# Three pairwise additions in place of one summing operation over the eight state terms

## The reference, cut to what matters

```
kv[i, j] = k[i] * v[j]                         # 8 x 8 products; here k = v, so 36 distinct pairs
out[i, j] = causal_conv(kv[i, j], kernel[h]) + kv[i, j] * D[h]
result[j] = sum over i = 0..7 of out[i, j] * q[i]
```

## Time and profile before

| what | value |
|---|---|
| median of 3 runs | 2442.73 us (2441.63 to 2445.28) |
| the profiled execution, its own time | 2441.71 us |
| its span, first to last instruction | 2439.9 us |
| busy in the span: PE, DVE, POOL | 2141.1 (88%), 1535.5 (63%), 949.3 us (39%) |
| mean granted TensorE clock | 0.936 |
| the summing operation, L1575 | 128 times, 267.3 us |

### The profile page before, as it was taken

The page is one execution under the profiler, slowest core; times in us unless marked ns, Lnnn a source line. Parts: engine busy times, 40 slices in busy tenths (PEclk is TensorE's granted clock), DMA queues, the critical chain, the costliest instruction groups (busy, mean ns, idle before and its releaser), DMA issues.

```text
span 2439.9 us, 32911 instructions
## 1 busy us (share of the span) xinstructions
PE 2141.1 (88%) x10954; PEld 1674.5 (69%) x10994; DVE 1535.5 (63%) x2567; ACT 1031.8 (42%) x1427; POOL 949.3 (39%) x774
## 2 busy tenths in 40 slices
PE   5989468888888645899999999999999999999898
PEld 4978445545455334688788688688688688688677
DVE  4866457776776558387488378478478477477411
ACT  3345344455545321533633543533533543443333
POOL 0100122333322021464464365365375375375263
PEclk9999789999999956799999999999999899999899
DMA  6656311111110021222322232232232232222231
GB/s 221 225 188 224 115 45 65 69 69 69 55 44 35 23 74 44 69 88 73 96 82 81 82 93 83 76 97 83 76 100 82 73 103 74 81 81 57 69 100 60
DMA packets 85161, 214.90 MB, mean 88 GB/s; under 512 B 7632, under 2 KB 9040, under 8 KB 79840
## 3 DMA queue, kind: packets, MB, share of 16 engines
q1 hardware_dynamic: 84800, 214.01, 26.8%
q10 hardware_dynamic: 288, 0.09, 0.0%
HBM read 180.52 MB, written 33.55 MB: 88 GB/s over the span
## 4 chain that ended last, share of the span: by engine, by line
PE 47%; issue 6%; DVE 6%; ACT 3%; POOL 2%; DMA 1%; ACTq 0%; SPq 0%; DVEq 0%; POOLq 0%
PE e_ps_u L52 4%; PE e_ps_u L53 4%; PE e_ps_u L54 4%; PE e_ps_out L52 4%; PE e_ps_out L54 4%; PE e_ps_out L53 4%; PE e_ps_g L52 3%; PE e_ps_g L53 3%; PE e_ps_g L54 3%; PE e_ps_m L52 3%; PE e_ps_m L54 3%; PE e_ps_m L53 3%; PE e_ps_m L1753 1%; DVE e_x3T L1575 1%; DVE e_kv_lo L1547 1%
## 5 line engine op out<-in xcount | busy, mean ns | idle before, releaser
L1232 POOL TENSOR_TENSOR e_gu_lo<-e_gu_raw,e_gu_hi 128x1024 fp32r<-128x1024 f32 (+1 forms) x128 | 272.0, 2125 | 414.1 <-ACT e_gu_hi L1315 412.3
L1575 DVE TENSOR_REDUCE e_x3T<-e_zp 128x128 f32<-128x1024 f32 x128 | 267.3, 2088 | 4.4
L1515 DVE SCALAR_TENSOR_TENSOR e_hd<-e_ps_u,vecs,e_sgw 128x512 f32<-128x512 f32 x96 | 71.9, 749 | 279.0 <-POOL e_sgw L1246 169.2
L52 PE MATMUL e_ps_out<-e_hd_hi,e_dn_hi 128*128 128x512 f32 x512 | 209.6, 409 | 0.0
L52 PE MATMUL e_ps_u<-e_xn_hi,e_gu_hi 128*128 128x512 f32 x512 | 209.0, 408 | 0.6 <-DVE e_hd L1515 0.6
L53 PE MATMUL e_ps_u<-e_xn_lo,e_gu_hi 128*128 128x512 f32 x512 | 206.0, 402 | 0.0
L54 PE MATMUL e_ps_u<-e_xn_hi,e_gu_lo 128*128 128x512 f32 x512 | 205.7, 402 | 0.0
L54 PE MATMUL e_ps_out<-e_hd_hi,e_dn_lo 128*128 128x512 f32 x512 | 204.9, 400 | 0.0
L53 PE MATMUL e_ps_out<-e_hd_lo,e_dn_hi 128*128 128x512 f32 x512 | 204.4, 399 | 0.0
L52 PE MATMUL e_ps_m<-e_kv_hi,e_t_hi 128*128 128x288 f32 x592 | 179.6, 303 | 22.6 <-DVE e_kv_lo L1547 16.9
L1237 POOL TENSOR_TENSOR e_dn_lo<-e_dn_raw,e_dn_hi 128x512 fp32r<-128x512 f32 x128 | 174.4, 1363 | 40.3 <-ACT e_dn_hi L1321 40.3
(11 more groups left out here) (288 smaller groups left out, 5417.5 us busy)
## 6 DMA issues: line engine op xcount, KB each, us to landing
e_gu_raw<-in_mgu SPq DMA_DIRECT2D x96, 512.0 KB, 3.3
e_dn_raw<-in_md SPq DMA_DIRECT2D x128, 256.0 KB, 3.1
stage<-in_x SPq DMA_DIRECT2D x8, 1024.0 KB, 6.9
c<-in_ctxT SPq DMA_DIRECT2D x8, 1024.0 KB, 5.6
raw_w<-in_w1T SPq DMA_DIRECT2D x8, 1024.0 KB, 4.8
raw_w<-in_w2T SPq DMA_DIRECT2D x8, 1024.0 KB, 7.4
gates<-gate SPq DMA_DIRECT2D x8, 1024.0 KB, 4.8
vals<-val SPq DMA_DIRECT2D x8, 1024.0 KB, 3.9
```

Of the source, the lines that this page charges most:

```text
L52: nc.tensor.matmul(out, w_hi, x_hi, start=first, stop=False, skip_group_check=skip)
L1232: nc.gpsimd.tensor_tensor(gu_lo[:, s % 2, a], gu_raw[:, s % 2, a], f32(gu_hi[:, s % 2, a]), ALU.subtract).then_inc(gulo_done, 1)
L1515: nc.vector.scalar_tensor_tensor(out=hd[:], in0=ps_u[:], scalar=vecs[:, V_BU + s:V_BU + s + 1], in1=sgw[:], op0=ALU.add, op1=ALU.mult).the ...
L1575: nc.vector.tensor_reduce(x3T[:, lb].rearrange("p (b n) -> p b n", b=B)[:, :, hh * CD:(hh + 1) * CD], zv(5, (1, 8), (21, 8)), AX.X, ALU.ad ...
```

## The change

The reduction of L1575 becomes three tensor additions on the same tile: four pairs of terms in place (512 numbers per partition), two pairs in place (256), and one pair into x3T (128). A new semaphore, tree_done, orders them. All eight terms lie in zp as before. Elsewhere the diff only merges semaphores that one engine counts up in a row, with the waits' numbers changed to match; no instruction other than the sum is added, removed or moved.

```diff
@@ experts_block, vector engine, unit()
             dve.wait_ge(prod_done, START + 4 * (v + 1))
-            nc.vector.tensor_reduce(x3T[:, lb].rearrange("p (b n) -> p b n", b=B)[:, :, hh * CD:(hh + 1) * CD],
-                                    zv(5, (1, 8), (21, 8)), AX.X, ALU.add).then_inc(red_done, 1)
+            nc.vector.tensor_tensor(zv(5, (21, 4), (1, 8)), zv(5, (21, 4), (1, 8)), zv(5 + 84, (21, 4), (1, 8)), ALU.add).then_inc(tree_done, 1)
+            dve.wait_ge(tree_done, START + 2 * v + 1)
+            nc.vector.tensor_tensor(zv(5, (21, 2), (1, 8)), zv(5, (21, 2), (1, 8)), zv(5 + 42, (21, 2), (1, 8)), ALU.add).then_inc(tree_done, 1)
+            dve.wait_ge(tree_done, START + 2 * v + 2)
+            nc.vector.tensor_tensor(x3T[:, lb].rearrange("p (b n) -> p b n", b=B)[:, :, hh * CD:(hh + 1) * CD],
+                                    zv(5, (1, 8)), zv(5 + 21, (1, 8)), ALU.add).then_inc(red_done, 1)
...
@@ setup_block: ghi_done is merged into hi_done
-        dve.wait_ge(ghi_done, 1)
+        dve.wait_ge(hi_done, len(cuts) + 1)
...
@@ scores_block: mask_done, abs_done, ahi_done become mask_step
-            dve.wait_ge(mask_done, h + 1)
+            dve.wait_ge(mask_step, 3 * h + 1)
...
@@ attn_block: amax_done is merged into qs_done, hmax_done into hs_done
-            act.wait_ge(qs_done, 10 * q + 5 * a + 5)
+            act.wait_ge(qs_done, 12 * q + 6 * a + 6)
...
-            act.wait_ge(hs_done, 4 * (4 * c + j + 1))
+            act.wait_ge(hs_done, 5 * (4 * c + j + 1))
```

More of the change, by code:

```diff
@@ L80, in setup_block @@
     ps_g = st.enter_context(nc.psum_tensor("ps_g", [P, 512], F32))
-    vecs_in, ident_in, wh_in, wht_in, wg_in, hi_done, lo_done, g_done, ghi_done = (
-        sem(n) for n in ("vecs_in", "ident_in", "wh_in", "wht_in", "wg_in", "hi_done", "lo_done", "g_done", "ghi_done"))
+    vecs_in, ident_in, wh_in, wht_in, wg_in, hi_done, lo_done, g_done = (
+        sem(n) for n in ("vecs_in", "ident_in", "wh_in", "wht_in", "wg_in", "hi_done", "lo_done", "g_done"))
     cuts = [(raw_wht, wht_hi, wht_lo, wht_in), (raw_wh, keep["wh_hi"], keep["wh_lo"], wh_in),
@@ L103, in _ @@
         act.wait_ge(g_done, 1)
-        nc.scalar.activation(keep["g_hi"][:], ps_g[:].rearrange("p (h d) -> p h d", h=HEADS), ACT.Copy).then_inc(ghi_done, 1)
+        nc.scalar.activation(keep["g_hi"][:], ps_g[:].rearrange("p (h d) -> p h d", h=HEADS), ACT.Copy).then_inc(hi_done, 1)
     @block.gpsimd
@@ L160, in scores_block @@
     names = ("x_in c_in stats_done mom_done rstd_done shift_done xn_done chi_done clo_done filled xhi_done qhi_done xnT_done "
[L161 removed]
+             "val_done gate_done q_done scores_done consts_done val_out gate_out mask_step const_in "
              "w1_in w2_in wohi_done wolo_done part_done sum_done mean_done scale_done scaled_done clip_done tern_done v0_in")
     (x_in, c_in, stats_done, mom_done, rstd_done, shift_done, xn_done, chi_done, clo_done, filled, xhi_done, qhi_done, xnT_done,
[L164 removed]
+     val_done, gate_done, q_done, scores_done, consts_done, val_out, gate_out, mask_step, const_in,
      w1_in, w2_in, wohi_done, wolo_done, part_done, sum_done, mean_done, scale_done, scaled_done, clip_done, tern_done, v0_in) = (
@@ L396, in _ @@
             dve.wait_ge(scores_done, START + HEADS * (NCH - 1) + h + 1)
-            nc.vector.tensor_tensor(gate[:, h], acc[:, h], keep["mask"][:, h], ALU.mult).then_inc(mask_done, 1)
-            dve.wait_ge(mask_done, h + 1)
+            nc.vector.tensor_tensor(gate[:, h], acc[:, h], keep["mask"][:, h], ALU.mult).then_inc(mask_step, 1)
+            dve.wait_ge(mask_step, 3 * h + 1)
             nc.vector.scalar_tensor_tensor(out=val[:, h], in0=gate[:, h], scalar=-1.0, in1=gate[:, h], op0=ALU.mult,
[L400 to L403, removed]
+                                           op1=ALU.max).then_inc(mask_step, 1)
+            dve.wait_ge(mask_step, 3 * h + 2)
+            nc.vector.tensor_scalar(keep["at_hi"][:, h], val[:, h], 1.0, None, ALU.max).then_inc(mask_step, 1)
+            dve.wait_ge(mask_step, 3 * h + 3)
             nc.vector.scalar_tensor_tensor(out=keep["at_lo"][:, h], in0=val[:, h], scalar=1.0, in1=f32(keep["at_hi"][:, h]),
@@ L506, in attn_block @@
      oT_done, og_done, z_done, zhi_done, zlo_done, wo_done, x1_done, stats_done, mom_done, rstd_done, rms_step,
-     r2_done, y_done, yg_done, amax_done, qs_done, round_done, yq_done, t_done, t_read, h_done, gelu_done,
-     hmax_done, hs_done, hround_done, hq_done, mm2_done, x2_done, x2_out, consts_done, dq2w_done, shift_done, held_done) = (sem(n) for n in (
+     r2_done, y_done, yg_done, qs_done, round_done, yq_done, t_done, t_read, h_done, gelu_done,
+     hs_done, hround_done, hq_done, mm2_done, x2_done, x2_out, consts_done, dq2w_done, shift_done, held_done) = (sem(n) for n in (
          "v_in gate_in x_in vhi_done vlo_done o_done ostats_done omom_done orstd_done oshift_done on_done "
          "oT_done og_done z_done zhi_done zlo_done wo_done x1_done stats_done mom_done rstd_done rms_step "
-         "r2_done y_done yg_done amax_done qs_done round_done yq_done t_done t_read h_done gelu_done "
-         "hmax_done hs_done hround_done hq_done mm2_done x2_done x2_out consts_done dq2w_done shift_done held_done").split())
+         "r2_done y_done yg_done qs_done round_done yq_done t_done t_read h_done gelu_done "
+         "hs_done hround_done hq_done mm2_done x2_done x2_out consts_done dq2w_done shift_done held_done").split())
     TU = 2 * TJ + 2
@@ L790, in pair_scale @@
             cols = slice(2 * a, 2 * a + 2)
-            n = 10 * q + 5 * a
+            n = 12 * q + 6 * a
             dve.wait_ge(yg_done, 4 * q + 2 * a + 2)
-            nc.vector.tensor_reduce(amax[:, cols], y[:, cols], AX.X, ALU.max, apply_absolute_value=True).then_inc(amax_done, 1)
-            dve.wait_ge(amax_done, 2 * q + a + 1)
+            nc.vector.tensor_reduce(amax[:, cols], y[:, cols], AX.X, ALU.max, apply_absolute_value=True).then_inc(qs_done, 1)
+            dve.wait_ge(qs_done, n + 1)
             nc.vector.tensor_scalar(amax[:, cols], amax[:, cols], 1e-5, None, ALU.max).then_inc(qs_done, 1)
-            dve.wait_ge(qs_done, n + 1)
+            dve.wait_ge(qs_done, n + 2)
             nc.vector.reciprocal(qrec[:, cols], amax[:, cols]).then_inc(qs_done, 1)
             nc.vector.tensor_scalar(dq1[:, cols], amax[:, cols], 1.0 / QMAX, keep["wmean"][:, 0:1], ALU.mult, ALU.mult).then_inc(qs_done, 2)
-            dve.wait_ge(qs_done, n + 4)
+            dve.wait_ge(qs_done, n + 5)
             nc.vector.tensor_scalar(qscale[:, cols], qrec[:, cols], QMAX, None, ALU.mult).then_inc(qs_done, 1)
@@ L815, in scale_h @@
             dve.wait_ge(gelu_done, START + 16 * c + 4 * j + 4)
-            nc.vector.tensor_reduce(hmax[:, col], h[:, j % 2], AX.X, ALU.max, apply_absolute_value=True).then_inc(hmax_done, 1)
-            n = 4 * (4 * c + j)
-            dve.wait_ge(hmax_done, 4 * c + j + 1)
+            nc.vector.tensor_reduce(hmax[:, col], h[:, j % 2], AX.X, ALU.max, apply_absolute_value=True).then_inc(hs_done, 1)
+            n = 5 * (4 * c + j)
+            dve.wait_ge(hs_done, n + 1)
             nc.vector.tensor_scalar(hmax[:, col], hmax[:, col], 1e-5, None, ALU.max).then_inc(hs_done, 1)
-            dve.wait_ge(hs_done, n + 1)
+            dve.wait_ge(hs_done, n + 2)
             nc.vector.reciprocal(hrec[:, col], hmax[:, col]).then_inc(hs_done, 1)
             nc.vector.tensor_scalar(dq2[:, col], hmax[:, col], dq2w[:], None, ALU.mult).then_inc(hs_done, 1)
-            dve.wait_ge(hs_done, n + 3)
+            dve.wait_ge(hs_done, n + 4)
             nc.vector.tensor_scalar(hscale[:, col], hrec[:, col], QMAX, None, ALU.mult).then_inc(hs_done, 1)
@@ L1642, in finish @@
                                                op1=ALU.add).then_inc(y_done, 1)
-        for s in (hdlo_done, stt_done, kvlo_done, tlo_done, prod_done, red_done, x3_done, xn_done, lg_done, wT_done, y_done):
+        for s in (hdlo_done, stt_done, kvlo_done, tlo_done, prod_done, tree_done, red_done, x3_done, xn_done, lg_done, wT_done, y_done):
             dve.sem_inc(s, START)
```

4 lines of the change are left out of this document (2 added, 2 removed).

## The result

The changed kernel takes 2469.35 us (median of 4 runs, 2464.37 to 2471.81) against 2442.18 us of the kernel before (4 runs). The ratio is 1.0108, 95% interval 1.0089 to 1.0126: 27 us, or 1.1%, slower. The forecast was 2459.5 us, range 2436 to 2484, with a chance of 0.65 for slower.

The account below looks back on a forecast made before the run. The DVE was taken to bound the opening, the PE the rounds. The opening's -7.0 us and the rounds' +23.8 made +16.8 us on the median 2442.73, about 2459.5 us, range 2436 to 2484.

Parts of the forecast that it names:

- The price alone: Every unit: three additions hold the DVE 1.40 us against the sum's 1.92, gaining 0.52 us where nothing interferes.
- Rival 3: Additions cost 2 ns a number like the strided reduction; opening loses 13 to 20 us, time about 2504; chance 0.07.
- the 1.0 for units 6 and 14: Opening: two units where the DVE already waits for the PE, so 2 by 0.52 us of gain comes off.
- The 0.3 taken off for the matrix cuts: Opening: 0.3 us less gain for three matrix cuts, where ACT waits for the PE as well.
- The mechanism: Rounds: operations with two SBUF inputs exclude each other, so each addition takes turns with POOL's; 3.4 us lost a round.
- The walk of steps 4 to 5: Rounds: additions queue behind POOL's operations, hd_lo ends at 1066.0, and PE's down of step 4 starts 1.1 us late.
- The walk of steps 7 to 8: Rounds: unit 7's additions queue behind POOL, so unit 8's products reach PE's unit 9 0.9 to 2.2 us late; 1.5 taken.
- late branch: Unit 7 to 8: POOL's sgw comes ahead of kv_lo, so unit 8's products end at 1101.3, 2.2 us late.
- For the rest ... I set 0.8 us, a choice and not a walk: Rounds: loss of 0.8 us a round set for units 1, 2, 5 and 11 to 13.
- rival 1: The rounds' margins absorb all delays and only the opening's gain counts: 2436 us; chance 0.17.
- rival 2: Turns fall well, about 1 us lost a round, 7 in all, cancelling the opening: 2438 to 2447 us; chance 0.18.
- rival 4: The same turns with POOL, but heavier: above 5.5 us a round, 2475 to 2490 us; chance 0.1.

## Why the prediction was right

**The pace.** The split into an opening paced by the DVE and rounds paced by the PE held. The kernel with neighbour reads shows both halves at once: 0.9 us less DVE time in every unit gave 11 us in the opening and left PE's wait for the products in the rounds, and the 107.9 us of the unit span, as they were.

**The price alone.** 0.69, 0.43 and 0.29 us were forecast and found. The opening's timeline shows the chain:

```profile
891.56 0.28 DVE L1572 TENSOR_TENSOR e_zp<-e_ps_m,e_qe 128x144 f32<-128x144 f32 x1
891.88 0.69 DVE L1575 TENSOR_TENSOR e_zp<-e_zp 128x512 f32<-128x512 f32 x1
892.61 0.43 DVE L1577 TENSOR_TENSOR e_zp<-e_zp 128x256 f32<-128x256 f32 x1
893.07 0.29 DVE L1579 TENSOR_TENSOR e_x3T<-e_zp 128x128 f32<-128x128 f32 x1
893.28 0.75 DVE L1547 TENSOR_TENSOR e_kv_lo<-e_kv_raw,e_kv_hi 128x576 fp32r<-128x576 f32 x1
```

893.28 - 891.88 = 1.40 us, the forecast to the hundredth. Rival 3 (2 ns a number) is refuted: these additions of runs of eight neighbours don't pay for the 84 bytes between the runs. The rule for reductions in the Trainium skill, page "VectorE: DVE Perf Modes", tier table (one element a cycle), holds for neighbours (1.22 us) and not for this kernel's access (2.10 us).

**The opening.** -7.0 us forecast, -8.2 measured. Of the 1.3 us that I took off the 8.3, the 1.0 for units 6 and 14 was too careful: DVE's waits for the PE there went from 1.4 us (two) to 0.6 (one), a gain of 0.8 instead. The 0.3 taken off for the matrix cuts was too little: the three waits for ACT went from 0.7 to 1.0 us each, 0.9 in all. 8.3 + 0.8 - 0.9 is the 8.2 measured. The granted clock of the opening rose from 0.72 to 0.76, which fits a PE that is late less often, but no run tests it.

**The rounds.** The mechanism held turn by turn. The walk of steps 4 to 5 had the three additions wait for gu_lo, dn_lo and sgw, and hd_lo for kv_raw; the timeline of the first round after (DVE, POOL, then PE's down of step 4) has the same turns, and answers to the earlier trace rows:

```profile
1050.07 2.16 DVE L1575 TENSOR_TENSOR e_zp<-e_zp 128x512 f32<-128x512 f32 x1
1052.27 1.41 DVE L1577 TENSOR_TENSOR e_zp<-e_zp 128x256 f32<-128x256 f32 x1
1053.71 1.27 DVE L1579 TENSOR_TENSOR e_x3T<-e_zp 128x128 f32<-128x128 f32 x1
1054.90 1.53 DVE L1520 TENSOR_TENSOR e_hd_lo<-e_hd,e_hd_hi 128x512 fp32r<-128x512 f32 x1
```

```profile
1049.29 2.40 POOL L1232 TENSOR_TENSOR e_gu_lo<-e_gu_raw,e_gu_hi 128x1024 fp32r<-128x1024 f32 x1 [4.88 <-ACT e_gu_hi L1315]
1051.64 1.75 POOL L1237 TENSOR_TENSOR e_dn_lo<-e_dn_raw,e_dn_hi 128x512 fp32r<-128x512 f32 x1
1053.36 1.47 POOL L1246 TENSOR_TENSOR e_sgw<-e_sg,e_wb 128x512 f32<-128x512 f32 x1
1054.79 1.09 POOL L1255 TENSOR_TENSOR e_kv_raw<-e_ke 128x512 f32<-128x512 f32 x1
```

```profile
1056.48 0.50 PE L52 MATMUL e_ps_out<-e_hd_hi,e_dn_hi 128*128 128x512 f32 x1 [0.83 <-DVE e_hd_lo L1520]
```

The first addition (0.69 alone) ends at 1052.2, half a microsecond behind gu_lo's end at 1051.7; dn_lo, 1.28 alone, takes 1.75; and so on down to hd_lo, which ends at 1056.43, and down starts at 1056.48. The walk of steps 7 to 8 came out on its late branch: POOL's sgw went in ahead of kv_lo (DVE's unit 7 to unit 8, POOL's sgw, PE's unit 9; answers to the earlier trace rows):

```profile
1084.57 2.79 DVE L1575 TENSOR_TENSOR e_zp<-e_zp 128x512 f32<-128x512 f32 x1
...
1089.64 1.85 DVE L1547 TENSOR_TENSOR e_kv_lo<-e_kv_raw,e_kv_hi 128x576 fp32r<-128x576 f32 x1
```

```profile
1089.40 1.47 POOL L1246 TENSOR_TENSOR e_sgw<-e_sg,e_wb 128x512 f32<-128x512 f32 x1 [0.89 <-ACT e_sg L1328]
```

```profile
1093.02 0.40 PE L52 MATMUL e_ps_m<-e_kv_hi,e_t_hi 128*128 128x288 f32 x1 [1.78 <-DVE e_zp L1572]
```

From the start of the first addition to its end are 2.8 us (walk: 2.8), to the end of kv_lo 6.9 (walk, late branch: 7.1). The run with one input shows that these waits come with the second input: there the three instructions never wait.

**The sizes in the rounds.** The forecast was 3.4 us a round, 23.8 in seven. Measured: 35.5 in seven, of which 33.5 in the unit spans, 4.8 a round, and 2 at the starts of the rounds. By the starts of PE's blocks in the first round, the changed kernel falls back by 0.4 us up to step 4, 1.0 at down of step 4 (forecast 1.1), 0.5 more up to unit 7, 1.95 at unit 9 (forecast 1.5, bounds 0.9 to 2.2), 0.1 up to unit 14 and 0.9 at unit 15. The two walked places hold. The term that was mis-sized is "For the rest ... I set 0.8 us, a choice and not a walk": it measures 1.9 us. The wait ahead of unit 15 and the spread of small delays are in it; a walk through the whole round would have been worth its time. The forecast of 2459.5 us is 10 us short, and this term (7 us in seven rounds) and unit 9 (3 us) are most of it.

**The clock, which the prediction didn't price.** Behind the first round, round times of the kernel before, by the addition of x, are 184.9 or 186.5 us; those of the changed kernel 191.2, six times running. From the start of unit 15 in one round to that of unit 0 in the next, where the PE waits for no products, both kinds of round are found in every kernel traced for this but one: 77.0 or 78.6 us in the kernel before, 78.5 each time in the changed one. The difference of 1.6 us sits behind the round's start. 16 us of it in three rounds, first the kernel before, then the changed one (the third figure from the end is the granted clock):

```profile
1191.70:1207.70 16.00, 15.87 (x59) 11.88 (x60) 2.47 (x5) 10.95 (x16) 7.11 (x5) 0.79 0.13 47
1376.60:1392.60 16.00, 15.80 (x53) 11.93 (x54) 2.46 (x5) 9.39 (x14) 7.11 (x5) 0.68 0.14 37
1563.00:1579.00 16.00, 15.73 (x59) 11.70 (x60) 2.59 (x6) 10.95 (x16) 7.12 (x5) 0.79 0.15 49
```

```profile
1185.00:1201.00 16.00, 14.89 (x50) 10.90 (x49) 2.75 (x10) 8.75 (x12) 6.02 (x5) 0.68 0.03 6
1376.20:1392.20 16.00, 14.89 (x50) 10.82 (x49) 2.78 (x10) 8.71 (x12) 5.96 (x5) 0.68 0.03 7
1567.40:1583.40 16.00, 14.89 (x50) 10.89 (x49) 2.74 (x10) 8.78 (x12) 6.00 (x5) 0.68 0.03 6
```

A granted clock of 0.68 against 0.79 over 16 us is 1.8 us of full-speed work. Which rounds get it differs from kernel to kernel, and even between kernels whose rounds hold nothing different. Against the kernel before, the stretches between the unit spans cost the changed kernel 5.7 us more in rounds 2 to 7, and the first round gets 3.7 us less of them behind the shorter opening: the 2 us above. PE's wait for e_xnat (1.5 us, L1797 before, L1801 after) is no second cause. In the kernel before, one of the two longer rounds has it (start at 1335 us) and the other doesn't (1892 us), and in the kernel with one-input instructions the one round that has it (1689 us) is a short one, 76.9 us from unit 15 to unit 0. That the clock makes the 1.6 us fits in size and place, but no run changed it alone.

**The rivals.** The margins do not take it all (rival 1, faster): PE's new waits say so. Small stalls that cancel the opening (rival 2) is what one addition in place of three gives. 4.8 us a round in the unit spans lies in the forecast's 2 to 5, at the end towards "heavier" (rival 4, above 5.5).

## What to carry to other kernels

Before a one-input operation is split into two-input ones, look at what GpSimd does at that time: in these traces operations with both inputs in SBUF take turns with its own, one-input reductions and products out of PSUM don't, and each of three short operations in a row can let a long one in. Read the price not from the sum of durations but at the few places where the bounding engine has less margin than one such turn; here 7 of 112 sets of additions made 14 of the 33.5 us. The same change gave 0.34% when kept to the opening and 0.58% when kept to the places where POOL was idle.

## What the runs showed of the hardware that I had not expected

A reduction of 1024 fp32 numbers takes 1.22 us when the numbers of a sum are 4 or 8 bytes apart and 1.97 to 2.19 us at 32, 64 and 84 bytes. Additions of runs of 8 neighbours with 84 bytes between the runs keep the short price (0.691 us for 512).

A wait of 1.8 us of an otherwise busy PE was followed by the lower clock level (matmuls of 288 columns 0.24 us apart, not 0.13) in the kernel with additions in unit 7 alone. It did so in five of that kernel's seven rounds and in three of seven with additions in the rounds only. In the changed kernel the same wait (1.76 to 1.79 us, 1.78 at 1093.02) was followed by it in none of seven: the granted clock is 1.00 in the 7 us behind each. None of the other eight kernels traced for this has the wait, and none shows the lower level between the starts of units 0 and 15. What decides whether the level falls stays open. A loss of about 1.6 us a round hangs on it.
